# Post-norm transformer layer on one core: another order of the pieces in phases 0 to 9 (output projection, V, attention product, norms, loads)

## The reference, cut to what matters

```python
# x: (16, 512, 256) fp32; 16 heads of 16; hidden width 1024
q = x @ wq + x @ Aq @ Bq * 4.0
k = x @ wk
v = x @ wv + x @ Av @ Bv * 4.0
q, k = apply_rope(q, sin, cos), apply_rope(k, sin, cos)
scores = where(causal, -1e9, einsum('bhqd,bhkd->bhqk', q, k) / sqrt(16))
x = layernorm(x + (softmax(scores) @ v) @ wo)
h = butterfly(x @ W_exp + b_exp, up_weights)              # 10 stages on 1024
h = butterfly(gelu(h + up_bias), down_weights)
x = layernorm(x + h @ W_con + b_con + down_bias)
```

## Time and profile before

| | |
|---|---|
| median of 3 runs | 1257.48 us (1255.92 to 1257.86) |
| the profiled execution, its own time | 1254.64 us |
| its span, first to last instruction | 1252.9 us |
| PE busy | 1112.8 us, 89% of the span |
| DVE, ACT, POOL busy | 871.8, 673.6 and 488.1 us |
| mean granted TensorE clock | 0.948 of full speed |

### The profile page before, as it was taken

How to read it: one execution, slowest core, us unless ns; L and a number is a source line. 1 busy time by engine, 2 the same in 40 slices (tenths; PEclk the granted TensorE clock), 3 DMA queues, 4 the chain that set the end, 5 groups by cost and what they waited for, 6 DMA issues and landing times.

```text
span 1252.9 us, 27672 instructions
## 1 busy us (share of the span) xinstructions
PE 1112.8 (89%) x8462; PEld 810.3 (65%) x8462; DVE 871.8 (70%) x1951; ACT 673.6 (54%) x1067; POOL 488.1 (39%) x539
## 2 busy tenths in 40 slices
PE   4677699999998989999998989999898999989877
PEld 3444377667676666767666766767666676767565
DVE  6679767676767676776768777676867677676332
ACT  2267566474745647473655647464664747465601
POOL 5334326352442535243352635244253524332310
PEclk9778799999999999999999999999999999999889
DMA  7763445545454565545445564545455455541110
GB/s 253 183 180 105 141 109 163 142 143 146 120 170 116 165 137 158 127 142 148 117 151 132 161 144 138 146 119 160 117 167 144 145 130 141 156 119 55 53 60 17
DMA packets 94983, 169.90 MB, mean 136 GB/s; under 512 B 14872, under 2 KB 36120, under 8 KB 94944
## 3 DMA queue, kind: packets, MB, share of 16 engines
q1 hardware_dynamic: 93888, 166.53, 48.6%
q10 hardware_dynamic: 832, 1.83, 0.4%
q0 software_dynamic: 224, 1.04, 0.2%
HBM read 92.28 MB, written 77.07 MB: 135 GB/s over the span
## 4 chain that ended last, share of the span: by engine, by line
PE 56%; DVE 17%; issue 10%; DMA 7%; ACT 4%; POOL 2%; SPq 2%; DVEq 0%; ACTq 0%; POOLq 0%
PE ps_m L550 18%; PE ps_m L699 13%; PE ps_m L669 8%; PE ps_m L598 5%; DVE m_raw L895 4%; PE ps_t L641 4%; DMA m_scr<-m_row 3%; PE ps_m L678 3%; DVE stats L949 2%; PE ps_m L684 2%; DVE y L964 2%; DMA q_st<-m_scr 2%; DVE m_raw L890 2%; PE ps_m L627 2%; ACT pT L771 1%
## 5 line engine op out<-in xcount | busy, mean ns | idle before, releaser
L771 ACT ACTIVATE pT<-ps_t 128x512 f32<-128x512 f32 x640 | 330.4, 602 | 232.6 <-PE ps_t L641 231.0
L895 DVE TENSOR_REDUCE m_raw<-ps_m 128x1 f32<-128x512 f32 (+2 forms) x768 | 338.3, 504 | 98.7 <-PE ps_m L627 95.0
L1036 POOL TENSOR_SCALAR_AFFINE_SELECT pT<-pT 128x512 f32<-128x512 f32 (+1 forms) x320 | 174.8, 553 | 393.5 <-ACT pT L771 393.5
L699 PE MATMUL ps_m<-w,gact 128*128 128x256 f32 x1024 | 235.3, 384 | 1.1 <-ACT gact L841 1.1
L699 PEld LDWEIGHTS ps_m<-w,gact 128*128 128x128 f32 x1024 | 190.7, 190 | 29.7 <-ACT gact L841 1.5
L598 PE MATMUL ps_m<-k_st,q_st 48*128 48x512 f32 (+3 forms) x1024 | 152.4, 353 | 42.7 <-DVE rope_in L914 18.2
L669 PE MATMUL ps_m<-pT,v_aug 128*32 128x512 f32 (+3 forms) x2048 | 156.2, 447 | 2.0 <-POOL pT L1036 1.4
L598 PEld LDWEIGHTS ps_m<-k_st,q_st 48*128 48x128 f32 x1024 | 88.8, 190 | 102.8 <-issue 87.1
L641 PE MATMUL ps_t<-q_st,k_st 50*128 50x512 f32 (+3 forms) x1024 | 128.3, 354 | 7.4 <-DMA q_st<-m_scr 5.6
L669 PEld LDWEIGHTS ps_m<-pT,v_aug 128*32 128x32 f32 x2048 | 58.5, 112 | 86.1 <-issue 79.5
L942 DVE TENSOR_TENSOR y<-ps_m,y 128x256 f32<-128x256 f32 x64 | 27.2, 425 | 121.7 <-PE ps_m L699 121.7
(11 more groups left out here) (106 smaller groups left out, 1678.9 us busy)
## 6 DMA issues: line engine op xcount, KB each, us to landing
qk_scr<-rot_hi SPq DMA_DIRECT2D x64, 512.0 KB, 3.6
q_st<-qk_scr SPq DMA_DIRECT2D x128, 192.0 KB, 4.7
k_st<-qk_scr SPq DMA_DIRECT2D x128, 192.0 KB, 5.1
qk_scr<-rot SPq DMA_DIRECT2D x32, 512.0 KB, 3.2
o_scr<-o_raw SPq DMA_DIRECT2D x64, 256.0 KB, 3.6
r_b<-in_xT SPq DMA_DIRECT2D x17, 512.0 KB, 7.4
o_c<-o_scr SPq DMA_DIRECT2D x32, 256.0 KB
r_b<-r_scr SPq DMA_DIRECT2D x32, 256.0 KB
```

What stands on the lines that cost most here:

```text
L699: mm = pe.matmul(pm[:, 0:D], gact[:, k, n * P:(n + 1) * P], w2[:, k, :], start=(k == 0), stop=(k == NHT - 1))
L771: act.activation(pT[:, g % 2, slot, half * T:(half + 1) * T], ps_t[:, ST_BANK[2 * n + r], :], ACT.Exp, scale=SCALE).then_inc(exp_done, 1)
L895: ins = dve.tensor_reduce(m_raw[:, r, u // 2, qt:qt + 1], scores[:, off:off + (qt + 1) * P], AX.X, ALU.max, negate=True)
L1036: pool.affine_select(out=v, in_=v, compare_op=ALU.is_ge, fill=0.0, base=0, pattern=pattern, channel_multiplier=-1).then_inc(mask_done, 1)
```

## The change

It reorders `steps` and adds two places to put steps: `between(p)`, between the last `ST` and the second `S` of a phase, and `last(p)`, behind `SEL`. No instruction is added or taken away and none changes its shape; nothing outside `steps` is touched. The parts:

- PE: `W2` 2 moves from phase 4 to 3, `W2` 3 from 5 to 4, `WO` 1 from 6 to 5, `V` 1 from 7 to 6, `PV` 1 from phase 6 to the front of phase 7, ahead of `XT`.
- First norm: statistics of both halves and the aggregation behind the `S` pieces of phase 5, the scaling `LNB` between the two `S` of phase 6.
- Second norm: `LNS` 3 from 5 to 7, `LNA` 1 from 6 to 8, `LNB` 2 and 3 and `OUT` from 7 to 9.
- Division: `RCP` and `REC` 1 from the end of phase 3 to between `W2` 1 and `W2` 2; `RCP` 0 from 8 to 9, behind `PV` 2; `ON` 0 from the end of 9 to the end of the next 0.
- POOL and DMA: `BIAS` behind `ROPE`, `SEL` and `ON` of phase 0; `XTL`, `XHI`, `XLO` one phase earlier; in phase 1 `RAW` and `MOUT` ahead of `QKH` and `XRES` behind; `SMOC` 0 from 7 to 8.

```diff
--- before.py
+++ after.py
@@ -68,23 +68,19 @@
 
         if p == 0:
             put("FILL", i, 3)
-            put("BIAS", i - 2, 0)
-            put("BIAS", i - 2, 1)
             if static and i == -1:
                 gemm("QK", 0, 0)
             gemm("QK", i + 1, 1)
             for n in range(5, 8):
                 gemm("W1", i - 2, n)
         elif p == 1:
-            put("XRES", i - 1, 0)
-            put("XRES", i - 1, 1)
+            gemm("QK", i + 1, 2)
+            gemm("PV", i - 1, 3)
             put("HIGH", i + 1, 0)
             put("LOW", i + 1, 0)
-            put("QKH", i + 1, 0)
-            gemm("QK", i + 1, 2)
-            gemm("PV", i - 1, 3)
             put("RAW", i - 1, 3)
             gemm("MT", i, 1)
+            put("QKH", i + 1, 0)
             put("MROW", i, 1)
         elif p == 2:
             put("VC", i)
@@ -99,9 +95,13 @@
                 gemm("V", 0, 0)
                 gemm("V", 0, 1)
             gemm("W2", i - 2, 1)
+            put("RCP", i - 1, 1)
+            put("REC", i - 1, 1)
+            gemm("W2", i - 2, 2)
+            put("RB", i - 1, 1)
         elif p == 4:
             put("QKL", i + 1, 1)
-            gemm("W2", i - 2, 2)
+            gemm("W2", i - 2, 3)
             gemm("MT", i, 2)
             gemm("PV", i, 0)
             put("ON", i - 1, 1)
@@ -109,25 +109,22 @@
             put("FILL", i + 1, 0)
             put("RAW", i, 0)
         elif p == 5:
-            gemm("W2", i - 2, 3)
             gemm("WO", i - 1, 0)
+            gemm("WO", i - 1, 1)
             put("FILL", i + 1, 1)
         elif p == 6:
-            gemm("WO", i - 1, 1)
-            put("LNS", i - 1, 1)
-            put("LNA", i - 1, 0)
             if not static or i >= 0:
                 gemm("V", i + 1, 0)
+                gemm("V", i + 1, 1)
             gemm("MT", i, 3)
-            put("LNB", i - 1, 0)
-            put("LNB", i - 1, 1)
+            put("MROW", i, 3)
+        elif p == 7:
             gemm("PV", i, 1)
-        elif p == 7:
+            put("RAW", i, 1)
             gemm("XT", i - 1, 0)
             gemm("XT", i - 1, 1)
-            if not static or i >= 0:
-                gemm("V", i + 1, 1)
         elif p == 8:
+            put("SMOC", i, 0)
             for n in range(4):
                 gemm("W1", i - 1, n)
         else:
@@ -135,45 +132,58 @@
             gemm("QK", i + 2, 0)
             gemm("MT", i + 1, 0)
             put("MROW", i + 1, 0)
+            gemm("PV", i, 2)
+            put("RCP", i, 0)
+            put("REC", i, 0)
             put("RB", i, 0)
-            gemm("PV", i, 2)
+
+    def between(p):
+
+        if p == 6:
+            put("LNB", i - 1, 0)
+            put("LNB", i - 1, 1)
 
     def late(p):
 
         if p == 0:
             put("ROPE", i + 1, 0)
             put("GE", i - 2, 1)
+        elif p == 1:
+            put("XRES", i - 1, 0)
+            put("XRES", i - 1, 1)
         elif p == 2:
             put("ROPE", i + 1, 1)
             put("SMOC", i - 1, 1)
-        elif p == 3:
-            put("RCP", i - 1, 1)
-            put("REC", i - 1, 1)
-            put("RB", i - 1, 1)
         elif p == 4:
             put("LNS", i - 2, 2)
+            put("XTL", i + 2, 0, B + 1)
         elif p == 5:
-            put("XTL", i + 2, 0, B + 1)
+            put("LNS", i - 1, 0)
+            put("LNS", i - 1, 1)
+        elif p == 6:
+            put("XHI", i + 2, 0, B + 1)
+        elif p == 7:
             put("LNS", i - 2, 3)
-            put("LNS", i - 1, 0)
-        elif p == 6:
-            put("LNA", i - 2, 1)
-            put("MROW", i, 3)
-            put("RAW", i, 1)
-        elif p == 7:
+            put("XLO", i + 2, 0, B + 1)
+            put("FILL", i + 1, 2)
+        elif p == 8:
+            put("GE", i - 1, 0)
+        elif p == 9:
+            put("RAW", i, 2)
             put("LNB", i - 2, 2)
             put("LNB", i - 2, 3)
-            put("SMOC", i, 0)
-            put("XHI", i + 2, 0, B + 1)
-            put("FILL", i + 1, 2)
             put("OUT", i - 2)
+
+    def last(p):
+
+        if p == 0:
+            put("ON", i - 1, 0)
+            put("BIAS", i - 2, 0)
+            put("BIAS", i - 2, 1)
+        elif p == 5:
+            put("LNA", i - 1, 0)
         elif p == 8:
-            put("GE", i - 1, 0)
-            put("XLO", i + 2, 0, B + 1)
-            put("RCP", i, 0)
-            put("REC", i, 0)
-        elif p == 9:
-            put("RAW", i, 2)
+            put("LNA", i - 2, 1)
 
     for p in range(NU // 2):
         early(p)
@@ -186,12 +196,12 @@
         put(*ahead[0])
         put("ST", i, t)
         put("ST", i, t + 1)
+        between(p)
         put(*ahead[1])
         late(p)
         put("SEL", i, t)
         put("SEL", i, t + 1)
-        if p == NU // 2 - 1:
-            put("ON", i, 0)
+        last(p)
         for when, at, kind, first, count in SETUP_UNITS:
             if static and (i, p) == (when, at):
                 for k in range(first, first + count):```

The lines of the changed kernel lie 10 further down. Three places show what moved.

TensorE, loop body, phase 6 into 7, before (`wv_hi,xT_hi` begins a piece of V, `m_pad` is `MT` 3, `pT,v_aug` is `PV` 1, `k_st,q_st` an `S`, `q_st,k_st` an `ST`, `ident,x_res` is `XT`):

```order
L678 MATMUL ps_m<-wo,o_c 128x256 x4
...
L550 MATMUL ps_m<-wv_hi,xT_hi 128x256 x2
...
L661 MATMUL ps_m<-ident,m_pad 128x128
...
L669 MATMUL ps_m<-pT,v_aug 32x512 x4
...
L598 MATMUL ps_m<-k_st,q_st 128x512 x2
...
L641 MATMUL ps_t<-q_st,k_st 128x512 x2
...
L598 MATMUL ps_m<-k_st,q_st 128x384 x2
...
L684 MATMUL ps_m<-ident,x_res 128x128 x4
...
L550 MATMUL ps_m<-wv_hi,xT_hi 128x256 x2
```

## The result

| | before | changed |
|---|---|---|
| median of the runs | 1257.67 us (1255.92 to 1262.42, 4 runs) | 1243.76 us (1243.20 to 1246.34, 4 runs) |
| profiled execution, span | 1252.9 us | 1244.6 us |
| PE busy | 1112.8 us | 1127.5 us |
| mean granted TensorE clock | 0.948 | 0.932 |

What follows compares the result with a forecast made beforehand. PE, busy 89% of the span, was taken as the bound, losing time to idle waits and a lower clock. Terms -1.7 - 1.35 + 0.25 - 0.4 - 0.39 = -3.6 us an iteration, -45 in all, gave 1212 us, range 1196 to 1237.

Steps and rivals of the forecast that it cites:

- the scaling in phases 5 to 8: First norm's scaling on DVE: 1.30 us, plus 0.4 for meeting two POOL selects of phase 6.
- The clock: Behind `XT`: idle pieces this small leave the clock high, so the low clock's 0.79 us an iteration comes back.
- my second rival: Clock stays low or falls more often through short stalls in phases 5 to 8: 1222 to 1265 us, chance 9%.
- my term of -1.7: Phases 5 to 8: `W1` 0 comes 16.2 us after the first `WO`, 1.7 us earlier an iteration.
- the stretch of `W1` 3: Phase 8: with the second norm's scaling moved away, the wait for `W1` 1's evacuation goes, -1.35 us an iteration.
- that of `ST` 5: Phase 2: `MOUT` goes first, `MROW` 1 leaves over 2 us earlier, and the wait goes, -0.39 us an iteration.
- `S` 1': Waits 0.3 us for the evacuation of `MT` 3, which now has the norm's statistics ahead of it.
- Phase 0: Its `S` waits some 0.25 us (0 to 1.7) for banks, as evacuations of `QK` 1 and `W1` 5 slip.
- The scaling of phase 9: Second norm's scaling in its new place meets selects of up to 0.64 us and takes 2.3 us.
- `QK` 2: Phase 1: 0.4 of the 0.96 us wait for its evacuation gained, between all 0.96 and a loss of 0.5.
- `RCP` 1 at nothing: Earlier `RCP` 1 brings `ON` 1 forward some 3 us, ahead of a `WO` that did not wait: no gain counted.

Runs made afterwards that it cites:

- the run with `XLO` late: The changed kernel with one step back in its old place, `XLO` at the end of phase 8 in place of 7: 1189.47 us, ratio to before 0.9455.
- the run with the split free: Changed kernel, `XLO` back in phase 8, first norm's first-half statistics between the two `WO`, `ON` 0 behind `ROPE`, `BIAS` and `XRES` later: 1184.04 us.
- the run with `PV` 1 ahead of the scores: Changed kernel with `XLO` back in phase 8 and `PV` 1 back in phase 6 ahead of the scores: 1224.22 us, ratio to before 0.9728.
- the reciprocal late: Changed kernel with `XLO` back in phase 8, and `RCP`, `REC` and `RB` 1 back at the end of phase 3: 1265.40 us, ratio to before 1.0066.

## Why the prediction was wrong

The direction was right and most of the waits went as counted; the sum was three times too large, because the largest term of it had the wrong sign.

- **The step that failed: the scaling in phases 5 to 8** ("To this I add 0.4 because the scaling meets the two selects of phase 6 on POOL"). I put it at 1.30 + 0.4 = 1.7 us. It took 3.72; 1.7 is what it takes when `XLO` is out of the way (1.70 in two runs). I had the mechanism, from `XLO` itself, but used it only for the norm that left phase 7. For the norm in phase 6 I counted two selects and never asked where `XLO`, moved by the same change, would run: it began 1.1 us after the scaling did. So the gap of 1.78 us ahead of `XT`, which I had at nothing, stayed at 1.85, worth 2.0 us an iteration.
- **The clock** ("I take it that pieces this small leave the clock high"). True of the small pieces, by the run with `XLO` late. But the gap was not small and the clock fell for 6.8 us: it cost 2.6 us an iteration, where I had the 0.8 of before as a gain. Part of my second rival came true, in cause not as put there: one long gap, not many short stalls. And the low stretch lies on scores and `W1` matmuls; before, 0.3 us of it fell into the gap and the rest on the narrow transposes and V. Together 2.0 + 2.6 us, 11 to 12 times: the 54 us by which the run with `XLO` late is faster.
- **The term itself, start to start.** From the first `WO` to `W1` 0 it was 17.86 us before, and my term of -1.7 makes it 16.2. In the changed kernel it is 18.78, in the run with `XLO` late 16.37:

```profile
646.19 3.72 PE L688 MATMUL ps_m<-wo,o_c 128*128 128x256 f32 x16
664.97 1.22 PE L560 MATMUL ps_m<-x1T_hi,w_hi 128*128 128x512 f32 x2
```

```profile
625.59 3.72 PE L688 MATMUL ps_m<-wo,o_c 128*128 128x256 f32 x16
641.96 0.73 PE L560 MATMUL ps_m<-x1T_hi,w_hi 128*128 128x512 f32 x2
```

- **The other terms, with `XLO` out of the way.** The same PE work lies between the same marks of the kernel before and of the run with `XLO` late, so their distances can be compared with my terms (us):

| stretch of PE | before | `XLO` late | gained | forecast |
|---|---|---|---|---|
| first `WO` to `W1` 0 | 17.86 | 16.37 | 1.49 | 1.7 |
| `W1` 0 to the first `S` behind `W1` 3 | 7.77 | 5.80 | 1.97 | 1.35 |
| to the first `S` of phase 0 | 14.33 | 14.35 | -0.02 | -0.25 |
| to the first `S` of phase 1 | 6.96 | 6.43 | 0.53 | 0.4 |
| to `W2` 1, over `ST` 5 | 8.57 | 7.96 | 0.61 | 0.39 |
| to the next first `WO` | 16.18 | 16.15 | 0.03 | 0 |

The sum is 4.6 (71.67 to 67.06) against my 3.6. The first row is 0.2 short of the forecast, since `S` 1' waits 0.71 us for `MT` 3 (I had 0.3). Phase 0 does not wait. The largest difference is with the waits that went: the stretch of `W1` 3 became 0.6 us shorter than by the idle time shown (1.37), that of `ST` 5 0.2 (0.37 shown). So the idle time in the profile was less than what a stall cost here; that I took the one for the other is a second error, of 0.8 us, and it hid in the total. What fills the difference stays open. That 1189 is below my 1212 is therefore not a success of the forecast.

- In the changed kernel the wait of `W1` 3 is gone, as forecast. The scaling of phase 9 takes 2.01 us (I had 2.3). `QK` 2: 0.64 us left, 0.56 forecast; the run with the split free, where POOL is out of the way, takes that wait away, so its cause is shown. `ST` 5 no longer waits for `MROW` 1, as forecast.
- `RCP` 1 at nothing: the number did no harm by luck, the reason was wrong. I compared `ON` 1 with a `WO` of the old order; without the early reciprocal `WO` waits 2.94 us in the new one.
- The Trainium skill's rule on the shared interface (Trainium skill, SBUF — State Buffer, SBUF: two separate sides: whichever of the two engines starts first keeps it for the whole instruction) is borne out by both runs in which POOL was made to wait: the scalings fell from 3.72 to 1.70 us and from 3.73 to 1.54. The Trainium skill's warning of a clock that oscillates with short stalls (Trainium skill, TensorE: Matmul & The Clock Gate, A second HAM failure mode) is not seen here: with three stalls an iteration, 1.8 us in all, the clock stays at 1.00.

Not tried: the same with the selects out of the scaling's way; by 1.70 against 1.38 us it could give some 0.3 us an iteration (an estimate). Why the last 3 to 5 us of the best versions do not show is open too.

## What to carry to other kernels

When a step is moved, list what the other engines do beside its new place, not only beside the old one. Here a POOL instruction of 2.4 us made a DVE scaling 2.0 us longer, and a wait that kept the two apart was worth 49 us, more than the overlap it forbade. A gap on TensorE can cost more than its length: here 1.85 us of gap cost 2.0 by itself and 2.6 by the clock behind it, and useless matmuls in the gap priced the two apart. Price a removed stall by distances between marks as well as by the idle time shown: 1.97 us against 1.37 here. An edit "at nothing" is only that as long as its cover stands: check the cover in the new order.

## What the runs showed of the hardware

- The same gap brings a low stretch in one iteration and not in the next. In the run with `PV` 1 ahead of the scores every loop iteration idles 1.84 us ahead of `XT`; periods are 67.98 us at clock 1.00 and 70.06 and 70.42 at 0.95. In the kernel before, gaps of 1.78 us brought 3.4 us at 1.2 GHz, in the changed one 1.85 us brought 6.8 us, and in its first loop iteration 1.86 us brought none. So the gap is what the low stretch needs here (filled with matmuls, it never came), but the gap alone does not decide whether it comes or how long it is.
- Three kernels with quite different waits settle at the same period once the clock falls in every iteration: 71.67 us before, 71.65 changed, 71.7 with the reciprocal late. So an edit that saves 1 to 2 us in the loop may show nothing at all while the clock falls every time, as the 1.9 us of this change did. Why it is this number stays open; where only some iterations have a low stretch, as with `PV` 1 ahead of the scores, the period is another.
